# Two coefficient products moved behind the score division, and 27 of 32 chunks gated and normed during the recurrence

## What is computed

```python
def step(buf, q_i):                       # 960 steps, one after the other
    ki = concatenate([buf, zeros(B, 1, D)], axis=1)         # window of 64, and a zero row
    scores = einsum('bwd,d->bw', q_i[:, None, :] * ki, w2_w) + w2_b[0]
    alpha = softmax(scores, axis=1)
    v_i = einsum('bwd,bw->bd', ki, alpha)
    return concatenate([buf[:, 1:, :], v_i[:, None, :]], axis=1), v_i

v_local = concatenate([feature[:, :W, :], vs])              # feature is layernorm(x)
y = tanh(v_local) * feature + feature
x1 = x + layernorm(layer_norm(y, ln_g, ln_b))
h = layernorm(x1)                         # input of the second layer
```

## Time and profile before

| | us |
|---|---|
| median of 3 runs | 2812.13 |
| lowest, highest | 2804.04, 2821.11 |
| profiled execution, its own time | 2813.75 |
| its span | 2812.0 |
| busy: VectorE | 2212.6 (79%) |
| busy: ScalarE | 1285.9 (46%) |
| busy: TensorE | 1182.1 (42%) |
| busy: GpSimd | 288.5 (10%) |

### The profile page before, as it was taken

How to read it: one execution, slowest core, us unless ns; L and a number is a source line. 1 busy time by engine, 2 the same in 40 slices (tenths; PEclk the granted TensorE clock), 3 DMA queues, 4 the chain that set the end, 5 groups by cost and what they waited for, 6 DMA issues and landing times. The chain is left out here.

```text
span 2812.0 us, 40923 instructions
## 1 busy us (share of the span) xinstructions
PE 1182.1 (42%) x7272; PEld 524.0 (19%) x7272; DVE 2212.6 (79%) x16135; ACT 1285.9 (46%) x3230; POOL 288.5 (10%) x425
## 2 busy tenths in 40 slices
PE   3010000101010010101004887878877777788796
PEld 1000000000000000000001111224321333223365
DVE  5999999999999999999975799776767667765133
ACT  1333333333333333333360456657854675577742
POOL 0000000000000000000010020032123210311211
PEclk8555555555555555555555799889997898899898
DMA  5000000000000000000034021103120221000100
GB/s 138 1 1 1 1 1 1 1 1 1 1 1 1 1 1 1 1 1 1 1 75 99 1 57 31 20 22 90 33 45 21 68 52 32 23 22 28 42 1 23
DMA packets 80203, 66.31 MB, mean 24 GB/s; under 512 B 8702, under 2 KB 64808, under 8 KB 79944
## 3 DMA queue, kind: packets, MB, share of 16 engines
q1 hardware_dynamic: 76872, 57.40, 8.4%
q0 software_dynamic: 3072, 6.30, 0.7%
HBM read 34.77 MB, written 28.57 MB: 23 GB/s over the span
## 5 line engine op out<-in xcount | busy, mean ns | idle before, releaser
L1332 DVE TENSOR_REDUCE nm_half<-pair 128x2 f32<-128x1024 f32 x512 | 611.8, 1220 | 197.9 <-PE pair L1580 186.4
L209 ACT ACTIVATE ex<-row,nmax 128x65 f32<-128x65 f32 x960 | 336.1, 350 | 891.8 <-DVE row L274 799.3
L1220 ACT ACTIVATE pt<-pair 128x1024 f32<-128x1024 f32 x512 | 513.4, 1025 | 383.8 <-PE pair L1590 370.6
L269 DVE SCALAR_TENSOR_TENSOR junk<-ex,tab 128x65 f32<-128x65 f32 x2850 | 618.1, 220 | 1.8 <-issue 1.1
L389 PE MATMUL p_s<-tab,bdg 128*128 128x32 f32 x120 | 31.8, 406 | 809.5 <-DVE tab L274 809.5
L1556 PE MATMUL p_o<-pt,va 128*9 128x512 f32 x2048 | 299.3, 659 | 7.0 <-ACT pt L1220 7.0
L274 DVE SCALAR_TENSOR_TENSOR tab<-rz,raw 128x1 f32<-128x1 f32 (+1 forms) x1890 | 293.7, 155 | 8.5 <-issue 2.4
L286 DVE STREAM_SHUFFLE row<-tab 128x130 f32<-128x130 f32 x930 | 280.1, 301 | 10.9 <-issue 3.1
L1580 PE MATMUL pair<-ks,qs 48*128 48x512 bf16 x1024 | 210.3, 422 | 108.7 <-ACT pt L1220 55.2
L269 DVE DVE_READ_ACCUMULATOR junk<-ex,tab 128x1 f32 x2850 | 235.4, 83 | 0.7
L1590 PE MATMUL pair<-qs,ks 50*128 50x512 bf16 x1024 | 210.5, 415 | 54.8 <-ACT pt L1220 24.8
(11 more groups left out here) (253 smaller groups left out, 2008.1 us busy)
## 6 DMA issues: line engine op xcount, KB each, us to landing
parts_dram<-parts SPq DMA_DIRECT2D x48, 256.0 KB, 3.6
qs<-parts_dram SPq DMA_DIRECT2D x32, 192.0 KB, 4.8
ks<-parts_dram SPq DMA_DIRECT2D x32, 192.0 KB, 5.2
hid<-xs_dram SPq DMA_DIRECT2D x33, 128.0 KB, 2.1
ys_dram<-hid SPq DMA_DIRECT2D x33, 128.0 KB, 1.8
h_dram<-f SPq DMA_DIRECT2D x20, 128.0 KB, 2.6
x<-in_x SPq DMA_DIRECT2D x4, 512.0 KB, 8.8
w_W<-in_W SPq DMA_DIRECT2D x1, 2048.0 KB
```

What stands on the lines that cost most here:

```text
L209: nc.scalar.activation(ex[:, r % 2, :], row[:, r % 2, 1, :], ACT.Exp, bias=nmax[:, r % 2:r % 2 + 1], accum_out=z[:, r % 2:r % 2 + 1]).then ...
L269: nc.vector.scalar_tensor_tensor(junk[:, g, :], ex[:, k, :], CAP, tab[:, g, r:r + ROW], ALU.min, ALU.mult, accum_out=raw[:, g:g + 1]).then ...
L1220: nc.scalar.activation(pt[:, kt % 2, :, tokens(t)], pair[fill.pair][:, :, :], ACT.Exp, scale=SCALE).then_inc(s_exp, 1)
L1332: nc.vector.reduce_max(nm_half[:, t, hp % 2, :, q], pair[fill.pair][:, :, :], AX.X, negate=True)\
```

## The change

Five things change.

1. VectorE's step: `weighted(0)` goes ahead of `largest`; `weighted(1)` goes behind the score division, so that both coefficient products stand between it and the shuffle.
2. ScalarE takes, between the exponentials of chunk c, work for chunks of `middle`: `gate` (tanh of chunk c) after step 6, three sums (`total`: Identity with an accumulator) after steps 13, 7 and 12, three sums of squares (`square`) after 17, 15 and 16, and three norm applications (`norm`) after 2, 3 and 5. The three are norm 0 of chunk c, norm 1 of chunk c - 1 and norm 2 of chunk c - 2.
3. GpSimd takes the rest: two operations of 128x128 for the gate (`gated`), two for gain and bias and one for the residual (`applied`), and the factors of the three norms on tiles of 3 columns: mean, variance, a first guess of the reciprocal root from its bits and three Newton rounds, and the shift, 17 operations, most with a wait for the one before (`link`). All of it stands between its copies and its wait for the chunk's last coefficient.
4. SyncE stores the 27 finished chunks one by one (`NORMED` = `NC` - 3) during the recurrence, four transfers each for `x1_dram` and `h_dram`; `g_row` and `b_row` are loaded at the start.
5. `middle` handles the 5 chunks that are left, in groups of 3 and 2, and no longer writes the fifth entry of `h_dram`.

```diff
@@ window_attention, block.sync
+            for k in range(NORMED):
+                sp.wait_ge(m_x1, k + 1)
+                for b in range(B):
+                    q = slice(L * b, L * b + L)
+                    sp.dma_start(x1_dram[b].rearrange("(k j) d -> j k d", j=L)[:, k, :], x[q, k, :]).then_inc(m_out, 16)
+                sp.wait_ge(m_h, k + 1)
...
+            sp.wait_ge(m_out, 16 * 2 * B * NORMED)
@@ block.gpsimd
+            def link(ins):
+                links[0] += 1
+                ins.then_inc(m_pool, 1)
+                pool.wait_ge(m_pool, links[0])
+            def applied(c):
+                for n, k in taking(c - 1):
+                    if n == 0:
+                        pool.wait_ge(m_norm, normed(c) - (1 if (1, k - 1) in taking(c - 1) else 0))
+                        link(nc.gpsimd.tensor_tensor(y[:, k % 2, :], y[:, k % 2, :], g_row[:, :], ALU.mult))
+                        nc.gpsimd.tensor_tensor(y[:, k % 2, :], y[:, k % 2, :], b_row[:, :], ALU.add).then_inc(m_affine, 1)
+                    elif n == 1:
+                        pool.wait_ge(m_norm, normed(c))
+                        nc.gpsimd.tensor_tensor(x[:, k, :], x[:, k, :], y[:, k % 2, :], ALU.add).then_inc(m_x1, 1)
+            def factors(c):
...
+                for i in range(3):
+                    link(nc.gpsimd.tensor_tensor(y_half[:, :], y_guess[:, :], y_guess[:, :], ALU.mult))
+                    link(nc.gpsimd.tensor_tensor(y_half[:, :], y_half[:, :], y_var[:, :], ALU.mult))
+                    link(nc.gpsimd.tensor_scalar(y_half[:, :], y_half[:, :], 1.5, None, ALU.add))
+                    link(nc.gpsimd.tensor_tensor((y_rstd if i == 2 else y_guess)[:, :], y_guess[:, :], y_half[:, :], ALU.mult))
...
+                applied(c)
+                if c < NORMED:
+                    gated(c)
+                if taking(c):
+                    factors(c)
                 pool.wait_ge(s_coef, L * (c + 1))
@@ block.scalar
+            def between(r, c):
+                for n, k in taking(c - 1):
+                    if r == (2, 3, 5)[n]:
+                        norm(n, k, c)
+                if r == 6 and c < NORMED:
+                    gate(c)
+                for n, k in taking(c):
+                    if r == (13, 7, 12)[n]:
+                        total(n, k)
+                    if r == (17, 15, 16)[n]:
+                        square(n, k, c)
@@ block.vector
+                    if not last:
+                        weighted(0, k, r, s_raw_score)
                     if not last:
                         largest(c, r + 1)
-                    if not last:
-                        weighted(0, k, r, s_raw_score)
                     if not last:
                         dve.wait_ge(s_raw_new, m)
                         dve.sem_inc(s_pace, 1)
                         dve.wait_ge(s_rz, n + 1)
                         divided(row[:, 1 - k, 1, WIN - 1:WIN].unsqueeze(2), 3, 4, k, s_new)
+                    if not last:
+                        dve.wait_ge(s_raw_score, m)
+                        divided(tab[:, 0:1, r + WIN:r + ROW], 0, 1, k, s_score)
                     if r:
                         dve.wait_ge(s_coef, n)
                     weighted(1, k, r, s_raw)
-                    if not last:
-                        dve.wait_ge(s_raw_score, m)
-                        divided(tab[:, 0:1, r + WIN:r + ROW], 0, 1, k, s_score)
                     weighted(2, k, r, s_raw)
@@ middle
-        G, GK = 4, NK // 4
+        starts = (NORMED, NORMED + 3, NK)
+        G, REST = len(starts) - 1, NK - NORMED
```

More of the change, by code:

```diff
@@ L10 @@
 U32 = mybir.dt.uint32
+I32 = mybir.dt.int32
 ALU = mybir.AluOpType
@@ L90, in window_attention @@
         raw = sb("raw", [P, 4])
+        g_row, b_row = xt["g_row"], xt["b_row"]
+        y = sb("y", [P, 2, D])
+        y_junk = sb("y_junk", [P, 6, D])
+        y_sum, y_sq, y_mean, y_guess, y_half, y_rstd, y_shift = (
+            sb(n, [P, 3]) for n in ("y_sum", "y_sq", "y_mean", "y_guess", "y_half", "y_rstd", "y_shift"))
+        y_var = sb("y_var", [P, 3])
         pf = ps("pf", [P, 2, 4 * P])
@@ L117, in window_attention, with taking, sums, rounds @@
             sem("s_g"), sem("s_bdg"))
+        m_w, m_out, m_pool, m_zero = sem("l_w"), sem("l_out"), sem("l_pool"), sem("l_zero")
+        m_tanh, m_y, m_sum, m_mean, m_sq, m_shift, m_norm, m_affine, m_x1, m_h = (
+            sem(n) for n in ("l_tanh", "l_y", "l_sum", "l_mean", "l_sq", "l_shift", "l_norm", "l_affine", "l_x1", "l_h"))
         block = ctx.enter_context(nc.Block())
+        def taking(c):
+            return [(n, c - n) for n in range(3) if 0 <= c - n < NORMED]
+        def sums(c):
+            return sum(len(taking(i)) for i in range(c + 1))
+        def rounds(c):
+            return sum(bool(taking(i)) for i in range(c + 1))
+        def normed(c):
+            return sum(n < 2 for i in range(c) for n, k in taking(i))
         @block.sync
@@ L129, in _ @@
             sp.dma_start(b0[:, :], io["w2_b"].rearrange("(d a) -> d a", a=1).broadcast_to((P, 1))).then_inc(s_w, 16)
+            sp.dma_start(g_row[:, :], io["ln_g"].rearrange("(a d) -> a d", a=1).broadcast_to((P, D))).then_inc(m_w, 16)
+            sp.dma_start(b_row[:, :], io["ln_b"].rearrange("(a d) -> a d", a=1).broadcast_to((P, D))).then_inc(m_w, 16)
             loaded = load_constants(sp, w, io, s_weights)
@@ L140, in _ @@
             sp.wait_ge(s_weights, loaded + 32 + 16)
+            for k in range(NORMED):
[4 more added lines that the diff above has]
+                sp.wait_ge(m_h, k + 1)
+                for b in range(B):
+                    q = slice(L * b, L * b + L)
+                    sp.dma_start(h_dram[b].rearrange("(k j) d -> j k d", j=L)[:, k, :], f[q, k, :]).then_inc(m_out, 16)
+            sp.wait_ge(m_out, 16 * 2 * B * NORMED)
         @block.gpsimd
@@ L227, in _ @@
                             .then_inc(s_bdg, 1)
+                    between(r, c)
         @block.vector
@@ L422, in ks, with chunks, done, wide @@
         def ks(g):
-            return slice(GK * g, GK * g + GK)
-        def wide(t):
-            return t[:, :].unsqueeze(1).broadcast_to((P, GK, D))
+            return slice(starts[g], starts[g + 1])
+        def chunks(g):
+            return range(starts[g], starts[g + 1])
+        def done(n, g):
+            return REST * n + starts[g + 1] - NORMED
+        def wide(t, g):
+            return t[:, :].unsqueeze(1).broadcast_to((P, len(chunks(g)), D))
         def pipelined(first, second):
@@ L470, in apply @@
                     act.wait_ge(m_shift, G * n + g + 1)
-                    for k in range(GK * g, GK * g + GK):
+                    for k in chunks(g):
                         nc.scalar.activation(out[:, k, :], src[:, k, :], ACT.Identity, bias=shift[:, k:k + 1],
@@ L503, in statistics @@
                     src = x if n == 2 else y
-                    for k in range(GK * g, GK * g + GK):
+                    for k in chunks(g):
                         nc.vector.bn_stats(stats[:, k, :], src[:, k, :]).then_inc(m_stats, 1)
-                    for k in range(GK * g, GK * g + GK):
-                        dve.wait_ge(m_stats, NK * n + k + 1)
+                    for k in chunks(g):
+                        dve.wait_ge(m_stats, REST * n + k - NORMED + 1)
                         nc.vector.bn_aggr(mv[:, k, :], stats[:, k, :]).then_inc(m_var, 1)
@@ L1732, in program @@
             xt["ident"], xt["eps"] = ident, eps
-            window_attention(nc, io, xt, w, stacks, s_weights, moe_dram)
+            for n in ("g_row", "b_row"):
+                xt[n] = first.enter_context(nc.sbuf_tensor(n, [P, D], F32))
+            window_attention(nc, io, xt, w, stacks, s_weights, moe_dram, x1_dram, h_dram)
             middle(nc, io, xt, x1_dram, h_dram)
```

67 lines of the change are left out of this document (52 added, 15 removed).

## The result

| | before, us | after, us |
|---|---|---|
| median of 4 runs | 2816.24 | 2736.26 |
| lowest, highest | 2804.04, 2821.11 | 2731.38, 2742.61 |
| profiled execution, its own time | 2813.75 | 2731.38 |

The ratio is 0.972, 95% interval 0.968 to 0.977. The prediction was 2736, range 2700 to 2785. The four executions of after took 2731.38, 2731.58, 2740.93 and 2742.61: the median lies between two pairs, and no execution took it.

A forecast was written before the change was run, and what follows sets the result against it. VectorE, or its loop with ScalarE, was taken to set the pace of the first layer's recurrence. The profiled 2813.75 - 63 - 44 + 31 = 2737.8, less 1.6 to the median, gave 2736 us, range 2700 to 2785.

The forecast's parts named there:

- order of VectorE: First layer's recurrence: reordering closes the gap before the shuffle, saving 0.07 us in each of 900 steps, 63 us.
- GpSimd beside the recurrence: Work added in 27 chunks holds up VectorE's two-input operations: 1.15 us per chunk, 31 us more.
- the products: GpSimd's five 128x128 operations per chunk beside the recurrence: 0.18 us each from VectorE, 0.9 us per chunk.
- small operations, stores, ScalarE's work: Added beside the recurrence: 17 three-column GpSimd operations at 0.015 us each, 0.25 per chunk; stores and ScalarE's work nothing.
- ScalarE's work: Between exponentials: an added activation and accumulator read (0.48 + 0.19 us) end at 1.11, before 1.24, so cost nothing.
- stage behind: Behind the recurrence: 5 chunks instead of 32 take 21.5 us instead of 65.2, 44 us gone.
- The gap: VectorE before the shuffle: 0.09 to 0.12 us lost per step to wake, increment and dispatch behind a late score division.
- The step of 1.24: Recurrence: exponentials 1.24 us apart after the reordering, instead of 1.31.
- the loop at 1.23: Recurrence: the loop through ScalarE's result sets a floor of 1.23 us per step once VectorE is faster.
- the increment at 0.01: ScalarE's increment between its waits for maximum and division, with the maximum later: 0.01 us per step.
- Rival 2: Recurrence: each of five GpSimd products blocks VectorE for its full 0.43 us, 58 us instead of 24, total 2770; chance 0.14.

The follow-up runs named there:

- experiment 1: The kernel before with only VectorE's new order, no work moved into the recurrence: 2750.88 us, ratio 0.979.
- experiment 6: The changed kernel with GpSimd's five 128x128 operations per chunk on 8 of 128 columns: 2704.22 us (one execution).
- experiment 5: The changed kernel with one Newton round instead of three, 9 small GpSimd operations per chunk instead of 17: 2739.94 us (one execution).
- Experiment 4: The kernel before, old order, without VectorE's counter increment between the wait for the score division and the shuffle: 2729.17 us (one execution).
- kernel 7: The changed kernel with each GpSimd copy and product held until the score division of its own step, some ScalarE work later: 2705.10 us, ratio 0.961.
- kernel 10: Kernel 7 without ScalarE's increment between its two waits and with the wait for the maximum written last: 2696.88 us (one execution).
- experiment 9: The changed kernel without ScalarE's counter increment between its waits for the maximum and the row division: 2769.59 us (one execution).
- experiment 8: Kernel 7 without the three counter increments per step, two on VectorE and one on ScalarE: 2720.40 us, ratio 0.966.
- experiment 11: Kernel 7 with VectorE's old order, no shuffle increment, GpSimd's work tied to the first coefficient product without its own increments: 2686.84 us, ratio 0.956.
- experiment 12: Experiment 11 with ScalarE's wait for the maximum written last and no increment between its two waits: 2684.66 us, ratio 0.956.
- experiment 2: The changed kernel with VectorE's old order, so only the work is moved: 2791.66 us, ratio 0.994.

## Why the prediction was right

| term, us | predicted | measured | from |
|---|---|---|---|
| order of VectorE | -63 | -61.7 | experiment 1 |
| GpSimd beside the recurrence | +31 | +30.9 | after less experiment 1 |
| of it the products | +24 | +29.8 | experiment 6 |
| of it small operations, stores, ScalarE's work | +7 | +1.1 | experiment 6 less experiment 1; experiment 5 |
| stage behind | -44 | -45.3 | after |
| start | 0 | -5.8 | after; not of the change, see below |
| second layer | 0 | -0.8 | after |

**The gap** was read rightly: a late producer, a wake, an increment, a dispatch. Experiment 4 takes the increment away and the gap closes with it; experiment 1 starts the chain earlier and it closes too. The step of 1.24 held: 1.22 from VectorE and ScalarE's loop, 0.02 from ScalarE's increment behind a later maximum (1.24 in kernel 7, 1.22 in kernel 10 of the list). I had put the loop at 1.23 and the increment at 0.01, between 0 and 0.06. What the prediction did not see is that the same reading names a cheaper cure: the increment need not be hidden, it can go.

**GpSimd's total** came out by two errors that cancel. A product costs 0.22, not 0.18. I had averaged over its place in the step, as if it fell anywhere. In the timeline above it doesn't, and the medians of the three steps say the same for the other chunks: ScalarE's norm or tanh runs right behind the exponential's accumulator read, GpSimd starts on its end, and so meets the table product and the row division (803.84 beside 803.86, 804.37 beside 804.44). The small operations cost nothing that can be seen, against 0.015 each. A GpSimd instruction of 8 columns takes 0.20 us and costs VectorE at most 0.01, one of 128 takes 0.45 and costs 0.22 more: what is paid for is the width. Rival 2, the full 0.43, is out in this kernel by the 0.22 of experiment 6; the rows agree, since VectorE's held instruction ended with GpSimd's or within 0.09 of it (804.29 and 804.38; 804.82 and 804.84) and had its own 0.15 to 0.22 in that time.

The Trainium skill (SBUF — State Buffer, Who interferes with whom) says that VectorE's two-input operations contend with GpSimd's reads, that a reduce doesn't, and that the order of issue decides who blocks. Experiment 7 agrees: the same products cost 0.03 at the shuffle and 0.22 at the divisions.

**ScalarE's work** costs nothing that can be seen (it is part of the 1.1 us), as predicted. An added activation of 0.48 and 0.19 fits behind the exponential; no table load stands between exponentials although a tanh does (the Trainium skill, ScalarE: Activation LUTs, Table sets, puts both into one set, and the trace agrees).

**The stage behind.** Predicted 21.5 us from the start of the stage, which was 1408.18 - 1404.09 = 4.1 behind the last exponential. Its tanh starts at 1371.64, again 4.1 behind, so 19.9 measured on that scale. The three norms up to the last stores took 14.6 instead of 15.5, those stores 3.7 instead of 3.5 (0.46 us each, not 0.57, but none of them early), and the load came 1.6 behind them instead of 2.5 (timeline of SyncE's queue):

```profile
1382.60 3.62 SPq L583 DMA_DIRECT2D x_dram<-x  x8
1386.26 3.72 SPq L583 DMA_DIRECT2D h_dram<-f  x8
```

**The start** is 5.8 us shorter without any part of the change in it. It consists of eight blocks, each with two matmuls of 512 columns. In the profiled execution of before such a pair takes 2.07 us up to the sixth block (30.78 is the second) and 1.13 only from 48.79 on; in that of after it is 1.13 from 30.55, the second block, on. First the two rows of before, then the one of after:

```profile
30.78 2.07 PE L358 MATMUL pq<-ft,wq 128*128 128x512 f32 x2 [0.68 <-ACT ft L200]
...
48.79 1.13 PE L358 MATMUL pq<-ft,wq 128*128 128x512 f32 x2 [0.68 <-ACT ft L200]
```

```profile
30.55 1.13 PE L492 MATMUL pq<-ft,wq 128*128 128x512 f32 x2 [0.68 <-ACT ft L290]
```

Over all fourteen traces the start follows the number of blocks with the long pair: one gives 50.4 and 50.6 us (after, experiment 6), three 51.8, four 53.4, six 56.1 and 56.2 (experiment 9, before), all eight 58.2 to 58.8 (the other eight). What decides on the block is not shown. The profile's PEclk does not tell it either: it says 1.00 for the whole start, but its first entry of the clock stands just where the short pairs begin (48.7 us before, 30.3 in after), and time ahead of the first entry counts as 1.00.

Without these 5.8 us the profiled execution of after would have taken 2737, against 2737.8 forecast before the step to the median. So the sum holds to about a microsecond on the profiled pair, by terms of which two were off by 5 to 6 us in opposite directions; the agreement of the medians to 0.3 us, between two pairs of executions 10 us apart, is luck.

**Left open.** Why the exponential starts only 0.05 after a wait that stands alone has ended, and 0.10 after the producer instead of 0.04, was not taken apart further than experiments 8 to 10. The same holds for the irregular longer steps. In experiments 11 and 12 the second layer, which they don't touch, took 1332.7 and 1333.6 us instead of 1337 to 1346; about 5 us of their gain are therefore not explained by the recurrence.

## What to carry to other kernels

Where a gap of about 0.1 us stands in front of an instruction in every turn of a loop, look at how late its producer is and what the program text has between the wait and the instruction; an increment without a reader there can cost more than a reordering of the engine brings. When an instruction has two waits, have the one that comes last be the one that it carries (here the one written first, where no increment stood between them), and look at the listing of instructions after every edit near it, since a deletion can swap them. Work given to GpSimd beside a loop through VectorE costs by its width and by the place in the step where it starts, so tie it to a VectorE signal just ahead of an instruction that reads one input.

## What the runs showed of the hardware that I had not expected

- An increment on VectorE between a late wait and the next instruction cost 0.09 us per step; between two waits on ScalarE 0.02 or nothing (experiments 4, 10, 12).
- Deleting ScalarE's increment made a step 0.04 longer, by the order of two waits alone (experiments 9, 10).
- GpSimd operations of 3 columns, 0.19 to 0.33 us each, cost VectorE nothing that can be told from noise (0.9 us for 232), and products of 8 columns at most 0.01 each (1.1 us for 135, with all the rest of the added work in it).
- PEclk for the recurrence reads 0.50 in some traces (before, after, experiments 2, 6, 9, 12) and 1.00 in the others, but TensorE was no faster there. In the others the first entry of the clock comes only behind the recurrence, and the matmul of each chunk that turns `vr` takes the same time, in the median 0.47 to 0.48 us in all fourteen traces. First a row of after (PEclk 0.50), then one of experiment 1 (1.00):

```profile
802.48 0.48 PE L510 MATMUL p_t<-ident,vr 128*128 128x128 f32 x1 [2.02 <-ACT vr L350]
```

```profile
834.57 0.48 PE L376 MATMUL p_t<-ident,vr 128*128 128x128 f32 x1 [2.02 <-ACT vr L217]
```
